# A row bound on the gathers and scatters of two routed layers in an audio tower on one Trainium2 core

## The chip, the core and the metric

The kernel is one program on one core of a Trainium2 chip. The metric is its device time in microseconds (us), from the first to the last instruction with the little that lies around it. One execution is also profiled; all stage times below are read from that one.

## What is computed

The reference is an audio tower on 64 clips of 33 frames (2112 tokens of 128 numbers): a windowed transform, then eight layers, each of which is added to the running sum `h`. The two layers that this change touches send each token to some of several small two-layer networks ("experts"):

```
# L1 ffn: 64 experts, each token goes to the 2 with the largest share
probs = jax.nn.softmax(logits, axis=-1)
vals, idx = jax.lax.top_k(probs, K)                 # K = 2
eh = jax.nn.silu(jnp.einsum('td,edf->tef', h, W1) + b1)      # 128 -> 512
eo = jnp.einsum('tef,efd->ted', eh, W2) + b2                 # 512 -> 128
moe = jnp.einsum('te,ted->td', combine, eo)
...
# L2 ffn: 8 experts, each token goes to 1
routes = jnp.argmax(probs, axis=-1)
h = jax.nn.gelu(xt @ w1 + bb1, approximate=False)
out = jnp.einsum('te,etd->td', onehot, y) * prob_max[:, None]
```

Only the chosen experts' results count, so the kernel computes those alone.

## The kernel before

Both layers are the function `moe`, called once with the key `sf` (64 experts, K = 2) and once with `gf` (8 experts, K = 1). Tokens are sorted by expert into slots, and slots are cut into tiles of `ST` = 128. A tile belongs to one expert, so an expert's last tile is filled only in part, and since the program can't know how the tokens will fall, it always runs the number of tiles that any routing could need: `NTILE` = 96 in the `sf` layer and 24 in the `gf` layer. There are K x 2112 real rows for them: 4,224 in 12,288 slots of `sf` (34%), and 2,112 in 3,072 slots of `gf` (69%).

A first block of `moe` computes the routing. Its last instructions, a chain on VectorE, make two index tables of int32 with a column of 128 for each tile: `take` (for each slot, the row of the token in the HBM tensor `token_rows`, `xs` in the code) and `give` (for each slot, the row of `expert_rows`, `ys`, that its result goes to). For an empty slot `take` is 0, so row 0 is fetched, and `give` is a row of its own behind the K x 2112 real ones, a trash row that nobody reads.

A second block runs the tiles, with every engine in its own program order and semaphores between them:

- SyncE loads the 514 KB of weights of tile j into `wb[:, j % 8]` (L1772), once tile j - 8 is done (`down`).
- GpSimd issues, for each j, an indirect DMA that gathers 128 rows of 512 bytes into `xi[:, j % 8]` (L2102), once the tile that held this buffer has been transposed (`turned`); and then, for tile d = j - 7 (`KEEP_RUN`), an indirect DMA that scatters the 128 rows of `yo[:, d % 8]` (L2107), once they are there (`y_ready`). So one gather and one scatter alternate, and a wait of either holds the other.
- TensorE transposes the gathered rows into `px` (L2131, which waits for the gather's landing, `taken`), and multiplies by the first weights into `ph` (L2139, 8 weight loads and matmuls as profiled) and the second into `po` (L2149, also 8).
- VectorE copies `px` to `xT` (L2199) and `po` to `yo` (L2205), ScalarE applies the activation (L2259, four a tile). VectorE also runs a small recurrence beside the `sf` tiles (L1637 to L1642), and in the `gf` layer a preparation of later weights (L2940, L2944).

Behind the last tile SyncE waits for all scatters and reads the rows back (`gk`, L2093), and VectorE and TensorE weigh and sum them. Semaphores of a finished stage are cleared on GpSimd (L98).

Of the kernel before, what the change touches and what calls it, by code (L numbers as in the profile page):

```python
# [5 lines left out]
F32 = mybir.dt.float32  # L6
# [3 lines left out]
ALU = mybir.AluOpType  # L10
# [5 lines left out]
D = 128  # L16
# [52 lines left out]
def unique(nc, name):  # L69

    return f"{name}_{nc.next_id()}"
# [1621 lines left out]


ST = 128
UN = 8
KEEP_RUN = 7

# [34 lines left out]
def moe(nc, cst, a, key, x, out, pre, F, act_fn, prob, capacity=None, code=None, shared=None, beside=None, late=False):  # L1733
# [7 lines left out]
    full = [TT, NTT, E]  # L1741
    w_dram = a[key + "_w"]
    xs = nc.dram_tensor(unique(nc, "token_rows"), [NT, D], F32, kind="Internal").ap()
    ys = nc.dram_tensor(unique(nc, "expert_rows"), [NTILE * ST if late else K * NT + NTILE * ST, D], F32, kind="Internal").ap()
    iota, iota16, low, index, tri, trash = (cst[n] for n in ("iota", "iota16", "low", "index", "tri", "trash"))

    def tile(t):
# [6 lines left out]
    with ExitStack() as ctx:  # L1754
# [19 lines left out]
        with ExitStack() as c1:  # L1774
# [173 lines left out]
            def _(dve):  # L1948
# [93 lines left out]
                if K == 2:  # L2042
# [1 line left out]
                                                op0=ALU.mult, op1=ALU.add))  # L2044
                    link(v.tensor_scalar(inv[:, 1, :], inv[:, 1, :], NTT - 0.5, -float(NTT), ALU.is_ge, ALU.mult))
                    link(v.tensor_tensor(inv[:, 2, :], inv[:, 2, :], inv[:, 1, :], ALU.add))
                link(v.tensor_scalar(take[:, :], inv[:, 2, :], -float(NTT), 0.0, ALU.add, ALU.max))
                if not late:
                    link(v.tensor_scalar(inv[:, 0, :], inv[:, 0, :], 0.0, None, ALU.is_equal))
                    link(v.scalar_tensor_tensor(out=inv[:, 1, :], in0=trash[:, 0:NTILE], scalar=float(K * NT + KB - 1), in1=inv[:, 0, :],  # L2050
                                                op0=ALU.add, op1=ALU.mult))
                    link(v.scalar_tensor_tensor(out=give[:, :], in0=inv[:, 1 + K, :], scalar=-float(KB), in1=inv[:, 1, :],
                                                op0=ALU.add, op1=ALU.add))

        with ExitStack() as c1:
            xi = sbuf(nc, c1, "xi", [ST, UN, D])
# [12 lines left out]
                stage(nc, "turned xT_ready up h_ready down y_ready shares_turned shares_kept"))  # L2069
            (weighed, added_up, dc) = c1.enter_context(stage(nc, "weighed added_up dve_chain"))  # L2070
            loaded = [s.sem for s in cst["y_back"]] if late else c1.enter_context(stage(nc, " ".join(f"loaded{g}" for g in range(NG))))
            pt = [t[:, b, :] for t in (px, ph, po) for b in range(2)]
            taken = [(s.sem, s.n) for s in x_in]
            given = [(s.sem, s.n) for s in y_out]
# [20 lines left out]

            @block.gpsimd
            def _(pool):
                for j in range(NTILE + KEEP_RUN):
                    if j < NTILE:
                        if j >= UN:  # L2100
                            pool.wait_ge(turned, j - UN + 1)
                        pool.indirect_dma_start(xi[:, j % UN, :], None, xs,  # L2102
                                                bass.IndirectOffsetOnAxis(ap=take[:, j:j + 1], axis=0)).then_inc(taken[j % UN][0], 16)
                    d = j - KEEP_RUN
                    if d >= 0 and not late:
                        pool.wait_ge(y_ready, d + 1)
                        pool.indirect_dma_start(ys, bass.IndirectOffsetOnAxis(ap=give[:, d:d + 1], axis=0), yo[:, d % UN, :],  # L2107
                                                None).then_inc(given[d % UN][0], 16)
                if late:
                    for j in range(NTILE - UN, NTILE):  # L2110
                        pool.wait_ge(*through(given, j))
                    for g, (t0, t1) in enumerate(groups):
                        for t in range(t0, t1):
                            pool.indirect_dma_start(gk[:, 0, t, :], None, ys,
                                                    bass.IndirectOffsetOnAxis(ap=place[:, t:t + 1], axis=0)).then_inc(loaded[g], 16)
# [1191 lines left out]
```

## Time and profile before

| | |
|---|---|
| median of 3 runs | 2192.21 us (2188.38 to 2197.41) |
| profiled execution: its own time / its span | 2194.47 us / 2192.5 us |
| TensorE, VectorE, ScalarE, GpSimd busy | 85%, 76%, 59%, 46% of the span |
| mean granted TensorE clock | 0.923 |
| gathers and scatters of the routed layers | 120 and 120, 0.99 and 1.00 us each on average on GpSimd |
| `sf` tiles: first gather issued / last scatter issued | 1164.05 us / 1411.68 us |
| `gf` tiles: the same | 1562.81 us / 1629.20 us |

The spans of an indirect DMA on GpSimd are the time in which that engine handles the instruction; its rows land later. "issue" as a releaser means that the engine waited for nothing that the profile shows. PEld is TensorE's weight load, which overlaps its matmuls.

### The profile page before, as it was taken

The numbers are of one execution on the slowest core, as the hardware profiler recorded it, in microseconds if no ns is written. First come the engines' busy times: TensorE is split into PE (matmuls) and PEld (weight loads), VectorE is DVE, ScalarE is ACT, GpSimd is POOL, SyncE is SP. The second block draws the span as 40 slices with busy tenths as digits, with TensorE's granted clock in tenths as the row PEclk, the third lists the DMA queues.
The fourth block names the chain that finished last, engine by engine and source line by source line (L and its number), as shares of the span: only waits on it lengthen the run. The fifth ranks groups of instructions, "written<-read, shape, count | busy, mean of one in ns | idle before, by whom it ended". The sixth has DMA issues, their size and how long they took to land. (4 is left out here: it accounts for less than half of the span.)

```text
span 2192.5 us, 49028 instructions
## 1 busy us (share of the span) xinstructions
PE 1853.0 (85%) x19401; PEld 1350.9 (62%) x19401; DVE 1665.2 (76%) x2535; ACT 1302.9 (59%) x2663; POOL 1006.3 (46%) x775
## 2 busy tenths in 40 slices
PE   7888888888888867897747887888688799999998
PEld 4444444444443333545537777767676599999997
DVE  3999999999999996678495443347544589989997
ACT  5777777776776655114334444343356488888886
POOL 1777777777677772110005777500350033333333
PEclk9899999999999999898668999999799699999999
DMA  3444444444444441520025888600750321111000
GB/s 128 148 130 130 126 150 129 130 131 125 126 131 144 135 133 49 129 43 1 17 97 155 268 258 251 189 10 5 246 157 14 149 85 63 70 59 66 16 4 23
DMA packets 91380, 242.16 MB, mean 110 GB/s; under 512 B 14800, under 2 KB 40000, under 8 KB 88720
## 3 DMA queue, kind: packets, MB, share of 16 engines
q1 hardware_dynamic: 82464, 218.66, 32.3%
q0 software_dynamic: 7680, 15.74, 3.0%
q10 hardware_dynamic: 1008, 4.62, 0.6%
q8 instruction: 154, 2.52, 0.5%
q14 instruction: 74, 0.61, 0.1%
HBM read 226.79 MB, written 12.19 MB: 109 GB/s over the span
## 5 line engine op out<-in xcount | busy, mean ns | idle before, releaser
L1099 POOL TENSOR_TENSOR dBu<-du,Bs 128x858 f32<-128x858 f32 (+1 forms) x240 | 589.7, 2459 | 212.8 <-DVE hst L1024 98.2
L568 PE MATMUL py<-hst,ident 128*128 128x429 f32 (+1 forms) x960 | 418.9, 568 | 94.8 <-DVE hst L1034 94.1
L1024 DVE TENSOR_TENSOR_SCAN hst<-dA,dBu 128x858 f32<-128x858 f32 (+1 forms) x240 | 457.7, 1907 | 19.3 <-ACT dA L873 15.8
L873 ACT ACTIVATE dA<-dt,negA 128x416 f32<-128x416 f32 (+1 forms) x480 | 269.4, 596 | 171.1 <-DVE hst L1024 168.4
L568 PEld LDWEIGHTS py<-hst,ident 128*128 128x128 f32 x960 | 185.8, 205 | 295.4 <-DVE hst L1034 167.7
L2855 POOL TENSOR_TENSOR hm<-h,mw 128x264 f32<-128x264 f32 x128 | 89.8, 701 | 391.2 <-DVE h L2836 391.2
L2102 POOL DMA_INDIRECT xi<-token_rows,take x120 | 118.8, 990 | 286.2 <-issue 278.0
L1034 DVE TENSOR_TENSOR hst<-hst,Cs 128x858 f32<-128x858 f32 (+1 forms) x240 | 246.9, 1029 | 0.0
L2259 ACT ACTIVATE eh<-ph,wb 128x128 f32<-128x128 f32 x480 | 136.3, 367 | 155.9 <-PE ph L2139 155.9
L2733 PE MATMUL pg<-hs,wh 128*128 128x66 f16 x6144 | 218.0, 193 | 5.8 <-issue 5.8
L2733 PE MATMUL pg<-xm,wi 128*128 128x66 f16 x6144 | 214.2, 195 | 4.8 <-issue 3.5
L2733 PEld LDWEIGHTS pg<-hs,wh 128*128 128x128 f16 x6144 | 203.9, 98 | 9.7 <-issue 6.3
L2733 PEld LDWEIGHTS pg<-xm,wi 128*128 128x128 f16 x6144 | 201.5, 98 | 9.3 <-issue 4.0
L2779 ACT ACTIVATE pg<-bz 128x1188 f32<-128x1188 f32 x128 | 149.1, 1165 | 6.2 <-PE pg L2728 2.2
L2107 POOL DMA_INDIRECT expert_rows<-yo,give x120 | 120.6, 1005 | 40.5 <-issue 32.6
L2205 DVE COPY yo<-po 128x128 f32<-128x128 f32 x120 | 34.9, 291 | 136.3 <-PE po L2149 136.1
L2139 PE MATMUL ph<-xT,wb 128*128 128x128 f32 x960 | 130.2, 280 | 2.8 <-DVE xT L2199 1.9
L2149 PE MATMUL po<-wb,eh 128*128 128x128 f32 x960 | 127.0, 276 | 0.0
L2826 DVE TENSOR_TENSOR prod<-z 128x528 f32<-128x528 f32 x128 | 111.3, 869 | 15.8 <-ACT z L2789 15.5
L2139 PEld LDWEIGHTS ph<-xT,wb 128*128 128x128 f32 x960 | 118.7, 194 | 4.0 <-DVE xT L2199 2.9
L2149 PEld LDWEIGHTS po<-wb,eh 128*128 128x128 f32 x960 | 117.4, 193 | 0.0
L2788 ACT ACTIVATE z<-pg,scale 128x528 f32<-128x528 f32 x128 | 88.1, 688 | 23.8 <-PE pg L2733 22.8
(487 smaller groups left out, 3209.4 us busy)
## 6 DMA issues: line engine op xcount, KB each, us to landing
wb<-sf_w SPq DMA_DIRECT2D x96, 514.0 KB, 5.0
Bs<-bc_rows SPq DMA_DIRECT2D x96, 429.0 KB, 4.6
Cs<-bc_rows SPq DMA_DIRECT2D x96, 429.0 KB, 3.5
mw<-route_weights SPq DMA_DIRECT2D x8, 2112.0 KB, 9.7
wb<-gf_w SPq DMA_DIRECT2D x24, 514.0 KB, 4.9
Bs<-bc_rows SPq DMA_DIRECT2D x24, 396.0 KB, 4.9
Cs<-bc_rows SPq DMA_DIRECT2D x24, 396.0 KB, 4.6
mb<-route_masks SPq DMA_DIRECT2D x8, 1088.0 KB, 12.4
```

The lines of the kernel that those rows point to most:

```text
L568: return nc.tensor.matmul(out, weight, moving, **kw)
L873: last = a(o, by_seq(dt[:, j % 2, h, 0:n])[:, :, 1:S], ACT.Exp, scale=negA[:, l, h * DST + k:h * DST + k + 1])
L1024: v.tensor_tensor_scan(hst[:, g % HR, 0:2 * n], dA[:, g % 2, 0:2 * n], dBu[:, g % 2, 0:2 * n], 0.0, ALU.mult, ALU.add).then_inc(h_ready, 1)
L1034: v.tensor_tensor(h, h, Cs[:, q % NBS, k % BG, 0:n].unsqueeze(1).broadcast_to([128, 2, n]), ALU.mult).then_inc(weighed, 1)
L1099: g_.tensor_tensor(dBu[:, g % 2, 0:2 * n].rearrange("p (a n) -> p a n", a=2), du[:, j % 2, :, 0:n], Bs[:, q % NBS, k % BG, 0:n].unsqueeze( ...
L2102: pool.indirect_dma_start(xi[:, j % UN, :], None, xs, bass.IndirectOffsetOnAxis(ap=take[:, j:j + 1], axis=0)).then_inc(taken[j % UN][0], 16)
L2107: pool.indirect_dma_start(ys, bass.IndirectOffsetOnAxis(ap=give[:, d:d + 1], axis=0), yo[:, d % UN, :], None).then_inc(given[d % UN][0], 16)
L2139: last = nc.tensor.matmul(ph[:, j % 2, f * ST:(f + 1) * ST], wb[:, j % UN, f * 128:(f + 1) * 128], xT[:, j % UN, :], start=True, stop=True)
L2149: last = nc.tensor.matmul(po[:, j % 2, 0:D], eh[:, j % 3, f, :], wb[:, j % UN, F + f * D:F + (f + 1) * D], start=(f == 0), stop=(f == FC - 1))
L2259: last = nc.scalar.activation(eh[:, j % 3, f, :], ph[:, j % 2, f * ST:(f + 1) * ST], act_fn, bias=wb[:, j % UN, W1 + W2 + f:W1 + W2 + f + 1])
L2733: return nc.tensor.matmul(pg[q][:, bank, c:c + CB], (wh if u else wi)[:, wp, q * HE + e, GO[z_] * D:(GO[z_] + 1) * D], rhs, start=False, s ...
L2779: a(pg[q][:, :, 0:PERB * CB], bz[:, q, :, :], ACT.Copy).then_inc(seeded[q], 1)
```

## The change

An empty slot's indices get 16384 added in both tables, which is above every row number, and both indirect DMAs get a bound (`bounds_check`: 2111 for the gather, K x 2112 - 1 for the scatter) with `oob_is_err=False`: rows whose index is above the bound are left out. `expert_rows` loses its trash rows. As the gather now leaves the empty slots' rows of `xi` as they were, `xi` is zeroed once before the tiles.

```
+SKIPPED = 16384.0
...
-    ys = nc.dram_tensor(unique(nc, "expert_rows"), [NTILE * ST if late else K * NT + NTILE * ST, D], F32, kind="Internal").ap()
+    ys = nc.dram_tensor(unique(nc, "expert_rows"), [NTILE * ST if late else K * NT, D], F32, kind="Internal").ap()
...
-                link(v.tensor_scalar(take[:, :], inv[:, 2, :], -float(NTT), 0.0, ALU.add, ALU.max))
-                if not late:
-                    link(v.tensor_scalar(inv[:, 0, :], inv[:, 0, :], 0.0, None, ALU.is_equal))
-                    link(v.scalar_tensor_tensor(out=inv[:, 1, :], in0=trash[:, 0:NTILE], scalar=float(K * NT + KB - 1), in1=inv[:, 0, :],
-                                                op0=ALU.add, op1=ALU.mult))
-                    link(v.scalar_tensor_tensor(out=give[:, :], in0=inv[:, 1 + K, :], scalar=-float(KB), in1=inv[:, 1, :],
-                                                op0=ALU.add, op1=ALU.add))
+                link(v.tensor_scalar(inv[:, 0, :], inv[:, 0, :], 0.0, SKIPPED, ALU.is_equal, ALU.mult))
+                v.scalar_tensor_tensor(out=take[:, :], in0=inv[:, 2, :], scalar=-float(NTT), in1=inv[:, 0, :], op0=ALU.add, op1=ALU.add)
+                link(v.scalar_tensor_tensor(out=give[:, :], in0=inv[:, 1 + K, :], scalar=-float(KB), in1=inv[:, 0, :],
+                                            op0=ALU.add, op1=ALU.add))
...
+            (cleared,) = c1.enter_context(stage(nc, "cleared"))
...
             @block.gpsimd
             def _(pool):
+                nc.gpsimd.memset(xi[:, :, :], 0.0).then_inc(cleared, 1)
+                pool.wait_ge(cleared, 1)
                 for j in range(NTILE + KEEP_RUN):
                     if j < NTILE:
                         if j >= UN:
                             pool.wait_ge(turned, j - UN + 1)
                         pool.indirect_dma_start(xi[:, j % UN, :], None, xs,
-                                                bass.IndirectOffsetOnAxis(ap=take[:, j:j + 1], axis=0)).then_inc(taken[j % UN][0], 16)
+                                                bass.IndirectOffsetOnAxis(ap=take[:, j:j + 1], axis=0),
+                                                bounds_check=NT - 1, oob_is_err=False).then_inc(taken[j % UN][0], 16)
                     d = j - KEEP_RUN
                     if d >= 0 and not late:
                         pool.wait_ge(y_ready, d + 1)
                         pool.indirect_dma_start(ys, bass.IndirectOffsetOnAxis(ap=give[:, d:d + 1], axis=0), yo[:, d % UN, :],
-                                                None).then_inc(given[d % UN][0], 16)
+                                                None, bounds_check=K * NT - 1, oob_is_err=False).then_inc(given[d % UN][0], 16)
```

In the order of the built program two places move. On GpSimd, at the head of the `sf` layer's tiles (`xi` is the gather's target, `expert_rows` the scatter's; ISA rows are semaphore clears), it stands before as

```order
L98 ISA x38
L2096 UNCONDITIONAL_BRANCH
L2102 DMA xi<-token_rows,take 128x128 x8
L2107 DMA expert_rows<-yo,give 16512x128
L2102 DMA xi<-token_rows,take 128x128
```

and in the change as

```order
L98 ISA x38
L2095 UNCONDITIONAL_BRANCH
L2097 MEMSET xi 128x1024
L2103 DMA xi<-token_rows,take 128x128 x8
L2109 DMA expert_rows<-yo,give 4224x128
L2103 DMA xi<-token_rows,take 128x128
```

The zeroing of all eight buffers comes ahead of the first gather, and the alternation behind it is as it was. These rows leave out what only sets a register: in the built program such an instruction, which holds the bound, now stands ahead of every one of the 240 indirect DMAs, and carries the wait that the DMA itself carried before.

On VectorE, at the end of the `sf` layer's routing block (`inv` is the scratch from which the tables are made), it stands before as

```order
L2046 TENSOR_TENSOR inv<-inv 128x96
L2047 TENSOR_SCALAR take<-inv 128x96
L2049 TENSOR_SCALAR inv<-inv 128x96
L2050 SCALAR_TENSOR_TENSOR inv<-trash,inv 128x96
L2052 SCALAR_TENSOR_TENSOR give<-inv 128x96
```

and in the change as

```order
L2046 TENSOR_SCALAR inv<-inv 128x96
L2047 TENSOR_TENSOR inv<-inv 128x96
L2048 TENSOR_SCALAR inv<-inv 128x96
L2049 SCALAR_TENSOR_TENSOR take<-inv 128x96
L2050 SCALAR_TENSOR_TENSOR give<-inv 128x96
```

Four instructions behind the last TENSOR_TENSOR on `inv` have become three.

## Rows read from the trace of the kernel before

**Rows 1.** Stages: busy time of each engine in three stretches

```profile
core 0: us, PE busy (x) PEld busy (x) DVE busy (x) ACT busy (x) POOL busy (x), PEclk, DMA share, GB/s
1175.00:1404.00 229.00, 188.31 (x1557) 176.84 (x1557) 91.76 (x343) 105.11 (x367) 174.66 (x179) 0.99 0.87 255
1562.00:1631.00 69.00, 58.02 (x461) 53.57 (x461) 35.60 (x76) 40.45 (x114) 51.68 (x48) 0.97 0.62 188
```

**Rows 2.** GpSimd in order of time: start, length; idle before and releaser

```profile
1164.05 1.17 POOL L2102 DMA_INDIRECT xi<-token_rows,take  x1 [100.10 <-issue]
...
1175.03 0.99 POOL L2107 DMA_INDIRECT expert_rows<-yo,give  x1 [1.07 <-DVE yo L2205]
1176.33 0.98 POOL L2102 DMA_INDIRECT xi<-token_rows,take  x1 [0.30 <-issue]
...
1400.92 0.99 POOL L2107 DMA_INDIRECT expert_rows<-yo,give  x1 [0.30 <-issue]
...
1405.45 0.97 POOL L2107 DMA_INDIRECT expert_rows<-yo,give  x1 [0.93 <-DVE yo L2205]
```

**Rows 3.** TensorE in order of time, 1202 to 1212 us

```profile
1202.42 0.27 PE L2131 MATMUL px<-ident,xi 128*128 128x128 f32 x1
...
1204.32 0.27 PE L2131 MATMUL px<-ident,xi 128*128 128x128 f32 x1
...
1206.22 0.27 PE L2131 MATMUL px<-ident,xi 128*128 128x128 f32 x1
...
1211.87 0.33 PE L2131 MATMUL px<-ident,xi 128*128 128x128 f32 x1 [3.60 <-DMA xi<-token_rows,take]
```

**Rows 4.** Waits from 1160 to 1400 us: total, times, longest

```profile
PEld px L2131 <- DMA xi<-token_rows,take: 52.9, 60, 3.8
```

**Rows 5.** DMA queues from 1170 to 1400 us (230 us), and issues

```profile
q1 hardware_dynamic: 12670, 46.32, 64.8%
q0 software_dynamic: 5683, 11.66, 21.5%
...
wb<-sf_w SPq DMA_DIRECT2D x88, 514.0 KB, 4.9
xi<-token_rows,take POOLq DMA_INDIRECT x92, 4.7
```

**Rows 6.** VectorE and TensorE at the border of routing and tiles

```profile
1160.06 0.21 DVE L2047 TENSOR_SCALAR take<-inv 128x96 int32<-128x96 f32 x1
1160.30 0.21 DVE L2049 TENSOR_SCALAR inv<-inv 128x96 f32<-128x96 f32 x1
1160.55 0.26 DVE L2050 SCALAR_TENSOR_TENSOR inv<-trash,inv 128x96 f32<-128x96 f32 x1
1160.84 0.26 DVE L2052 SCALAR_TENSOR_TENSOR give<-inv 128x96 int32<-128x96 f32 x1
...
1161.63 4.82 PE L133 MATMUL po<-ident 128*128 128x128 f32 x24 [4.34 <-PEq L1774]
```

**Rows 7.** Groups on GpSimd: busy, mean ns of one | idle before

```profile
L1080 POOL MEMSET whh<- 128x512 f32 x1 | 0.5, 527 | 0.0
...
L1077 POOL MEMSET edge<- 128x1 f32 x1 | 0.1, 104 | 0.0
```

**Rows 8.** SyncE's issue of weights: durations ns min/median/max

```profile
L1772 SPq MOVE wb<-sf_w x96: 29/29/42, 1133.4 to 1394.9; - x96
```

**Rows 9.** GpSimd, then VectorE, in the `gf` tiles in order of time

```profile
1584.46 0.99 POOL L2107 DMA_INDIRECT expert_rows<-yo,give  x1 [0.31 <-issue]
...
1605.46 1.90 POOL L2102 DMA_INDIRECT xi<-token_rows,take  x1 [0.30 <-PE px L2131]
```

```profile
1605.30 1.22 DVE L2944 TENSOR_TENSOR wi<-wf,wi 128x1024 f16<-128x1024 f32 x1
1607.20 1.22 DVE L2944 TENSOR_TENSOR wi<-wf,wi 128x1024 f16<-128x1024 f32 x1
```

**Rows 10.** Waits from 1560 to 1640 us

```profile
PE px L2131 <- DMA xi<-token_rows,take: 8.1, 7, 2.1
```

**Rows 11.** The gather over the whole span: durations ns min/median/max

```profile
L2102 POOL DMA_INDIRECT xi<-token_rows,take x120: 940/968/1898, 1164.0 to 1618.3; - x120
```

## The prediction

> **What bounds the kernel now.** I read the stages first, because the change touches only two stretches of the span. In the `sf` tiles (229 us of them in [rows 1]) TensorE is busy 82% of the time, GpSimd 76%, the DMA engines 87%, and no one number says who leads. The order of time on GpSimd does. From the first scatter at 1175.03 us to the scatter behind the last gather at 1400.92 us there are 88 pairs of one gather and one scatter: 225.9 / 88 = 2.57 us a pair, and it is made of 0.97 + 0.30 + 0.99 + 0.30 us [rows 2, 11], where 0.30 us is an idle time that recurs before nearly every one and has no releaser ("issue"). So GpSimd handles indirect DMAs without a pause. Its 76% is 100% with those gaps.
>
> TensorE, on the other hand, has time. Where rows are there it starts a tile every 1.90 us (1202.42, 1204.32, 1206.22), and then it waits 3.60 us for a gather [rows 3]; its wait for gathers is 52.9 us in the stretch [rows 4], near to 96 x (2.57 - 1.90) = 64 us. The `sf` tiles are paced by GpSimd's time for one instruction, and the next limit is TensorE at 1.90 us a tile. A third is close: the weights keep the sixteen DMA engines busy 64.8% of 230 us for 88 loads, 1.69 us a tile, and the indirect DMAs 21.5%, 0.54 us for one of the some 91 pairs [rows 5], together 2.23 us of 2.57.
>
> In the `gf` tiles GpSimd paces too, but only from about 1584 us on. TensorE is busy 58.0 of 69 us there [rows 1] and waits for gathers 8.1 us in all [rows 10].
>
> So the time of this change is decided by one number that the trace of before can't show: what GpSimd needs for an indirect DMA with a bound, of whose 128 indices only 44 (`sf`, 4,224 / 96) or 88 (`gf`) are in bounds.
>
> **The change part by part.**
>
> *Head of the tiles.* The zeroing of 128x1024 lies ahead of the first gather with nothing beside it that helps: TensorE's first transpose needs that gather. By the two MEMSET rows [rows 7] an element costs (0.527 - 0.104) / 511 = 0.83 ns, so 0.104 + 1023 x 0.00083 = 0.95 us, and one gap of 0.30 us: 1.25 us. VectorE ends its chain earlier: from the start of L2047 to the end of L2052 it takes 1.04 us [rows 6], and three instructions of this kind take 0.24 + 0.26 + 0.26 = 0.76 us, 0.28 us less, and the other engines enter the tiles 0.5 us behind that end. Net +1.0 us a layer, +2 us in both.
>
> *A register write before each DMA.* On SyncE a MOVE takes 29 ns [rows 8]. It costs nothing if GpSimd's sequencer does it while the previous DMA is handled, and 240 x 0.029 = 7.0 us if it adds to each gap, 6 us of that where GpSimd paces. A DMA that is released by a semaphore starts 0.28 us after it (1175.03 against the end of `yo`, and likewise at 1405.45 [rows 2]), as long as the gap between two that wait for nothing, so the sequencer seems not to be ahead. I take 5 us.
>
> *The DMA engines' load.* Rows moved fall to 34% in `sf`: 0.54 us a pair becomes 0.19, and the DMA engines' need falls from 2.23 to 1.88 us a tile. While GpSimd gives 2.57 us a tile, this alone buys nothing. It matters as the cover for a faster GpSimd: with it, a tile can come down to TensorE's 1.90 us, without it only to 2.23.
>
> *GpSimd's time for one instruction.* Call f the part of its 0.98 us (mean of 0.97 and 0.99) that goes with the number of rows actually issued. With f = 0 nothing changes. With f = 1 it would be 0.98 x 0.34 = 0.34 us in `sf`, and TensorE's 1.90 us would pace: 88 x 0.67 = 59 us less there, and up to 8 us in `gf` [rows 10]. No row shows a DMA with fewer rows, so f is open in both directions, a bound's test could cost as well. Two things lean on it. For a small f: a gather takes up to 1.90 us instead of 0.97 where VectorE's 1.22 us instructions with two inputs (L2944) run beside it [rows 9, 11]; something in it is held that is not the writing of rows' descriptors alone, and that stays. For a larger one: 128 rows on two sides in 0.97 us is 7.6 ns a row, as an instruction of 128x1 takes only 0.10 us [rows 7], so most of the 0.97 us is work that an almost empty instruction does not have. I take a third. Then an `sf` instruction takes 0.98 x (1 - 0.66 / 3) = 0.76 us, a pair 2 x (0.76 + 0.30) = 2.13 us, and 88 pairs save 88 x 0.44 = 39 us; in `gf` 0.98 x (1 - 0.31 / 3) = 0.88 us, and some 14 paced pairs save 14 x 0.20 = 3 us, of which I keep 2.
>
> A rule of the Trainium skill speaks against this (page DMA: Bandwidth & Descriptors, section Anatomy of one DMA): descriptor generation is a small part, and many descriptors can be emitted before their incremental cost is seen. By it f is near 0 and the sum would be that of the first rival below, +7 us; by the third that I took from the row it is -34 us. The same page names a fixed cost of some 2 us for a DMA's completion, which fewer rows would not shorten; the 4.7 us to landing in [rows 5] are in no conflict with it. On what holds the long gathers, SBUF — State Buffer, section Who interferes with whom, says that a VectorE instruction with two SBUF inputs blocks GpSimd's reads of SBUF, and here the trace agrees: 1.90 against 0.97 us.
>
> *Sum.* +2 (heads) +5 (register writes) -39 (`sf`) -2 (`gf`) = -34 us. The profiled execution took 2194.47 us (span 2192.5 and 2 around it), the median of the runs is 2192.21; the same difference on the median gives 2158 us. At the tail nothing is added: the last scatters wait for `yo` (0.93 us, [rows 2]), and SyncE reads back behind their landing as before.
>
> **The rivals.** About 0.5% (11 us) is what a measurement of this kernel tells from no change.
>
> *Nothing changes on GpSimd (f = 0).* The bytes go, but they were not the limit, and heads and register writes stay: +2 to +8, I take +7, 2199 us. For it: the load on the DMA engines is 87%, not 100%, and the rule above. Against it: the 7.6 ns a row. Chance 0.26.
>
> *The bound makes the instruction longer.* A test for each of 128 indices, or the loss of a form in which four rows of 512 bytes go as one packet (5683 packets for 11.66 MB are 2 KB each [rows 5]), adds d to each. 88 pairs and 14 in `gf` and the first 8 gathers: 0.1 us costs 0.1 x (176 + 28 + 8) = 21 us. On top of +7 it decides from d = 0.02 us on, at which the kernel is 11 us slower; with d = 0.2 us (1.6 ns an index) it is +49 us, 2241 us. For it: the pace hangs on this one instruction and nothing covers it. Against it: skipped rows save writes that are there now. Chance 0.31.
>
> *GpSimd gets faster, but the DMA engines don't get freer*, because skipped rows split packets: 2.23 us a tile would pace, 88 x 0.34 = 30 us less, -25 us with the rest, 2167 us. It lies within my own case.
>
> My case, GpSimd shorter, whatever the f between 0.1 and 1: chance 0.43, from 2192 + 7 - 67 = 2132 us to about 2181.
>
> **How the numbers follow.** The time is the likeliest case's, 2158 us; its own range is 2130 to 2181. For 8 in 10 the range has to take in f = 0 (up to 2203) and the slower case to d = 0.2: 2130 to 2245 leaves out about 0.03 below and 0.13 above. Faster by over 0.5% is my case, 0.43; the same is the first rival, 0.26; slower 0.31.
>
> **What would show it.** In the changed kernel's order of time on GpSimd: a MEMSET of about 0.95 us before the first gather; gathers and scatters in `sf` at 0.76 us for my case, 0.97 for the first rival, above 1.0 for the second; the gap still 0.30 or 0.33. The distance of two pairs in the middle of `sf` should be 2.13 us. The last 21 of 96 tiles are empty, by the number of tokens that each expert gets from the reference's inputs, so the instruction should be shortest there if it goes with the rows, and TensorE should run at 1.90 us. Bytes on queue 0 should fall to about 40% of 15.7 MB. TensorE's wait for gathers should fall from 52.9 us to some 20. The prediction is wrong if the instruction's time doesn't depend on the rows, or if it is longer with the bound whatever the rows.

## The result, and the profile after

The changed kernel took 2198.32 us (2192.67 to 2205.03) against 2192.17 us (2186.56 to 2199.86) for the kernel before, 20 executions of each: ratio 1.003, 95% interval 1.0021 to 1.0038. That is 6 us slower, inside the 0.5% that the prediction calls no change, and 40 us above the 2158 us that it gave. It was the first rival's time (2199 us), though not quite by the first rival's sum.

The page of the profile after shows that the rows did go. GpSimd's own row, the DMA totals, queue 0, and the two groups of indirect DMAs:

```profile
span 2196.8 us, 49270 instructions
PE 1852.0 (84%) x19401; PEld 1352.4 (62%) x19401; DVE 1665.2 (76%) x2533; ACT 1303.3 (59%) x2663; POOL 1016.7 (46%) x777
DMA packets 91382, 233.00 MB, mean 106 GB/s; under 512 B 16736, under 2 KB 42000, under 8 KB 88720
q0 software_dynamic: 7680, 6.58, 1.2%
L2109 POOL DMA_INDIRECT expert_rows<-yo,give x120 | 123.8, 1031 | 39.2 <-issue 27.5
L2103 POOL DMA_INDIRECT xi<-token_rows,take x120 | 124.3, 1036 | 37.7 <-issue 31.7
```

Before, queue 0 carried 7680 packets with 15.74 MB at 3.0% of the DMA engines. The bytes fell to 42%; the number of packets did not change at all. And an average gather or scatter takes *longer* than before: 1.04 and 1.03 us instead of 0.99 and 1.00.

The stages (answers to [rows 1]), the waits for gathers (to [rows 4]) and the queues of the `sf` tiles (to [rows 5]):

```profile
core 0: us, PE busy (x) PEld busy (x) DVE busy (x) ACT busy (x) POOL busy (x), PEclk, DMA share, GB/s
1175.00:1404.00 229.00, 181.68 (x1513) 170.31 (x1511) 89.82 (x334) 102.15 (x357) 176.32 (x173) 1.00 0.74 220
1562.00:1631.00 69.00, 58.89 (x458) 56.31 (x458) 35.30 (x76) 41.72 (x115) 49.64 (x46) 0.90 0.59 192
...
PEld px L2133 <- DMA xi<-token_rows,take: 59.7, 59, 2.9
...
q1 hardware_dynamic: 12632, 46.21, 67.0%
q0 software_dynamic: 5512, 4.28, 7.4%
...
wb<-sf_w SPq DMA_DIRECT2D x88, 514.0 KB, 4.3
xi<-token_rows,take POOLq DMA_INDIRECT x87, 3.5
```

The DMA engines' share fell from 0.87 to 0.74, queue 0's part of it from 21.5% to 7.4%, and a gather lands 3.5 us after its issue instead of 4.7. The transfers are fewer bytes and land sooner. Yet TensorE waits for gathers 59.7 us instead of 52.9, and fewer of its instructions fit into the same 229 us (1513 against 1557). Where the time sits is seen on GpSimd in order of time: the head of the tiles, two pairs from the middle, and the end, from the last gather on (answers to [rows 2]).

```profile
1159.22 0.95 POOL L2097 MEMSET xi<- 128x1024 f32 x1 [99.21 <-issue]
1161.06 1.23 POOL L2103 DMA_INDIRECT xi<-token_rows,take  x1 [0.90 <-POOL xi L2097]
...
1171.94 1.01 POOL L2109 DMA_INDIRECT expert_rows<-yo,give  x1 [0.53 <-issue]
...
1279.42 1.02 POOL L2103 DMA_INDIRECT xi<-token_rows,take  x1 [0.30 <-issue]
1280.75 1.02 POOL L2109 DMA_INDIRECT expert_rows<-yo,give  x1 [0.31 <-issue]
1282.07 1.02 POOL L2103 DMA_INDIRECT xi<-token_rows,take  x1 [0.30 <-issue]
1283.40 1.01 POOL L2109 DMA_INDIRECT expert_rows<-yo,give  x1 [0.31 <-DVE yo L2207]
...
1404.15 1.02 POOL L2103 DMA_INDIRECT xi<-token_rows,take  x1 [0.30 <-issue]
1405.48 1.02 POOL L2109 DMA_INDIRECT expert_rows<-yo,give  x1 [0.31 <-issue]
...
1410.83 0.98 POOL L2109 DMA_INDIRECT expert_rows<-yo,give  x1 [0.43 <-issue]
```

This order of time holds the prediction's own test. By the number of tokens that each expert gets, the last 21 of the 96 `sf` tiles have no row at all, and the instruction should have been shortest there if it went with the rows. The last gather (1404.15) takes 1.02 us, as do those in the middle; over the 21 empty tiles the mean is 1.022 us, over the filled ones from the tenth on 1.022 as well.

The durations of the gather, of the register write that now stands ahead of each, and of the scatter, over the whole span (answers to [rows 11]):

```profile
L2103 POOLq MOVE  x120: 29/29/35, 1160.2 to 1614.9; - x120
L2103 POOL DMA_INDIRECT xi<-token_rows,take x120: 995/1024/1675, 1161.1 to 1622.1; - x120
```

```profile
L2109 POOL DMA_INDIRECT expert_rows<-yo,give x120: 980/1016/1672, 1171.9 to 1634.4; - x120
```

Gathers went from a median of 0.97 to 1.02 us, scatters from 0.99 to 1.02. From the first scatter to the scatter behind the last gather it is 1405.48 - 1171.94 = 233.5 us for the same 88 pairs, 2.654 us a pair instead of 2.567, +7.7 us. The gaps are 0.30 to 0.31 as before: the register write is hidden. Laid out from the end of the chain that makes `give` to the read-back of `expert_rows` behind the last scatter, 252.9 us before (1161.10 to 1414.02) and 260.2 after (1157.18 to 1417.41):

| part of the `sf` tiles | before | after | difference |
|---|---|---|---|
| end of `give` to the first gather | 2.95 | 3.88 | +0.9 |
| first gather to first scatter | 10.98 | 10.88 | -0.1 |
| 88 pairs | 225.89 | 233.54 | +7.7 |
| scatter behind the last gather to the read-back | 13.10 | 11.93 | -1.2 |

The same stretch of the `gf` layer went from 72.8 to 74.7 us, +1.9, and VectorE's shorter chain returned 0.3 us a layer. These parts sum to about +9 us; the two profiled executions differ by 4.3 us, because in the one after everything ahead of the tiles happened to be 3.9 us shorter. The medians, +6 us, lie between.

### The profile page after: what moved, and what is told of

Its sections match the earlier page's. It is cut to its first block and busy times, and to the rows that moved or that the text cites. A ratio compares the mean times of both kernels' runs of the same rounds, so it can differ in the third digit from the quotient of the medians.

```text
span 2196.8 us, 49270 instructions
## 1 busy us (share of the span) xinstructions
PE 1852.0 (84%) x19401; PEld 1352.4 (62%) x19401; DVE 1665.2 (76%) x2533; ACT 1303.3 (59%) x2663; POOL 1016.7 (46%) x777
## 3 DMA queue, kind: packets, MB, share of 16 engines
q0 software_dynamic: 7680, 6.58, 1.2%
## 5 line engine op out<-in xcount | busy, mean ns | idle before, releaser
L2103 POOL DMA_INDIRECT xi<-token_rows,take x120 | 124.3, 1036 | 37.7 <-issue 31.7
```

Source lines behind the costliest of these rows:

```text
L2103: pool.indirect_dma_start(xi[:, j % UN, :], None, xs, bass.IndirectOffsetOnAxis(ap=take[:, j:j + 1], axis=0), bounds_check=NT - 1, oob_is_ ...
```

## Experiments

Behind each time stand, in brackets, its ratio to the kernel before on the same chip and the 95% interval of that ratio. Two kinds of chip occurred, two chips of each beside that of the result. On one kind the kernel before has a median of 2191 to 2193 us, as in the result above, on the other 2243 to 2245 us; an experiment is read only against its own chip. The first four kernels ran on one of the latter.

**1. The bound alone, with all rows moved.** The only edit on the kernel before is a bound that no index exceeds:

```diff
                         pool.indirect_dma_start(xi[:, j % UN, :], None, xs,
-                                                bass.IndirectOffsetOnAxis(ap=take[:, j:j + 1], axis=0)).then_inc(taken[j % UN][0], 16)
+                                                bass.IndirectOffsetOnAxis(ap=take[:, j:j + 1], axis=0),
+                                                bounds_check=NT - 1, oob_is_err=False).then_inc(taken[j % UN][0], 16)
...
-                                                None).then_inc(given[d % UN][0], 16)
+                                                None, bounds_check=K * NT + NTILE * ST - 1, oob_is_err=False).then_inc(given[d % UN][0], 16)
```

> The kernel before with a bound on both indirect DMAs that no index exceeds (trash rows, row 0 for empty slots and index tables as before, no zeroing): every one of the 128 rows still goes. Theory A, the bound's presence costs some 40 ns an instruction, whatever the rows: gathers about 1.02 and scatters 1.02 us in the sf tiles, a pair 2.65 us, +7 us in sf and +1 in gf, about 2200 us against 2192. Theory B, it is the skipping of rows that costs: 0.97 and 0.99 us, a pair 2.57 us, no change. Theory C, the bound costs more than 40 ns and the rows left out give part of it back: over 1.05 us an instruction, a pair over 2.70 us, over 2204 us.

**2. Every row of the gathers left out.** In the changed kernel all entries of `take` lie above the bound, so the experts compute on zeros:

```diff
-                v.scalar_tensor_tensor(out=take[:, :], in0=inv[:, 2, :], scalar=-float(NTT), in1=inv[:, 0, :], op0=ALU.add, op1=ALU.add)
+                v.scalar_tensor_tensor(out=take[:, :], in0=inv[:, 2, :], scalar=SKIPPED, in1=inv[:, 0, :], op0=ALU.add, op1=ALU.add)
```

> The changed kernel with every gather index above its bound, so that no gather moves a row (the tokens never reach the experts, whose results are those of zeros); scatters as in the change. Theory A (time by indices given, not by rows moved): gathers stay at 1.00 to 1.02 us, a pair at 2.65 us, 2198 us, although queue 0 loses the gathers' bytes. Theory C (time by rows moved): gathers fall below 0.95 us, and each 0.05 us is worth 4 us. Theory B (a skipped row costs extra): gathers above 1.05 us.

**3. The scatter alone.** The changed kernel with the gathers of before: no bound on them, no zeroing.

> Bound and left-out rows on the scatter alone; the gather as before, without zeroing. Theory A: gather 0.97, scatter 1.02 us, a pair 2.59 to 2.60 us, +2 to +3 us in sf, and -0.6 us at the heads: 2192 + 2 = 2194 us. If the effects of gather and scatter depended on each other (through the shared DMA queue) the gather would move from 0.97 too.

**4. Gathers of 64 indices.** In the changed kernel each gather takes partitions 0 to 63 only; rows 64 to 127 are not loaded.

```diff
-                        pool.indirect_dma_start(xi[:, j % UN, :], None, xs,
-                                                bass.IndirectOffsetOnAxis(ap=take[:, j:j + 1], axis=0),
+                        pool.indirect_dma_start(xi[0:64, j % UN, :], None, xs,
+                                                bass.IndirectOffsetOnAxis(ap=take[0:64, j:j + 1], axis=0),
```

> The changed kernel with gathers of 64 indices instead of 128: tokens in slots 64 to 127 of a tile are not gathered (zeros go through in their place). Theory A (an instruction's time goes with the number of indices that it is given): gather 0.5 to 0.65 us, a pair 2.2 to 2.3 us, some -33 us in sf, about 2160 us. If the time is nearly all fixed: gather 0.95 to 1.02 us, 2198 us.

Measured, before at 2243.2 us: 2256.52 (1.007, 1.0052 to 1.0088), 2262.03 (1.0074, 1.0051 to 1.0096), 2256.31 (1.0063, 1.0048 to 1.0078), 2260.1 (1.0078, 1.006 to 1.0096). The durations of the gather in the four, in this order, ns min/median/max:

```profile
L2102 POOL DMA_INDIRECT xi<-token_rows,take x120: 992/1024/1597, 1157.7 to 1676.4; - x120
```

```profile
L2103 POOL DMA_INDIRECT xi<-token_rows,take x120: 996/1027/1976, 1163.8 to 1683.4; - x120
...
q0 software_dynamic: 7680, 3.36, 0.6%
```

```profile
L2100 POOL DMA_INDIRECT xi<-token_rows,take x120: 940/973/2027, 1157.7 to 1676.7; - x120
```

```profile
L2103 POOL DMA_INDIRECT xi<-token_rows,take x120: 938/962/1727, 1159.6 to 1677.6; - x120
```

These four rows settle what GpSimd needs. With the bound a gather takes 1.02 to 1.03 us whether all 128 rows are moved (first), on average 44 (after) or none (second); in the third, which has the bound on the scatters alone, the gather is back at 0.97 and the scatter at 1.01. So an instruction with the bound takes 0.02 to 0.05 us longer, and the rows left out return nothing: f, the part that goes with the rows, is 0. Even half as many *indices* save only 0.06 us of 1.02. Queue 0 keeps its 7680 packets with 3.36 MB, when no gathered row is moved at all.

The times of these four are another matter. They are 13 to 19 us above their own chip's kernel before, where the longer instructions alone were expected to make +8 (1) or +2 (3). On this chip the `sf` tiles are not paced by GpSimd in the way of [rows 2]; I come back to it under 7.

**5. The changed kernel again, and the bound with reporting.** On a chip where before took 2191.93 us: the kernel before, the changed one, and the kernel of 1 with the bound's default, by which an index out of bounds is reported (there is none).

```diff
-                                                bounds_check=NT - 1, oob_is_err=False).then_inc(taken[j % UN][0], 16)
+                                                bounds_check=NT - 1).then_inc(taken[j % UN][0], 16)
```

> The kernel before itself, as a run with a trace of its own beside the kernels below: no difference. Its GpSimd rows (0.97 and 0.99 us, a pair 2.57 us) are the measure for the others of this call; if the sf tiles have waits here that its first trace did not have, they belong to the chip and not to a change.

> The changed kernel beside the kernel before on one chip, each with a trace. Theory A (the bound costs 40 ns an instruction and nothing is given back): +7 us in the sf pairs, +0.65 us at each head, -1 us at the tail, +6 us in all, 1.003 as before. If the four kernels of the first call were 0.6 to 0.8% slower for another reason (GpSimd waited there for yo up to 2.1 us), that wait should be seen in this trace and not in that of the kernel before.

> As the bound alone, but with out-of-bounds indices reported instead of left out (there are none). Theory A1, the check itself costs the 40 ns: 1.02 us an instruction again. Theory A2, the silent leaving-out is what costs: 0.97 and 0.99 us, no change.

Measured: 2191.3 (0.9993, 0.9979 to 1.0007), 2201.36 (1.0032, 1.002 to 1.0043), 2205.71 (1.0058, 1.0036 to 1.0079). The result repeats. The bound with all rows moved costs 14 us here: gathers 1.04, scatters 1.03 us at the median, 2.686 us a pair, 88 x 0.12 = 10.5 us in `sf` alone. So the slower kernel needs no rows left out to be explained. Nor is it the silent form that costs: with reporting a gather is no shorter, but 0.02 us longer than in the changed kernel.

**6. Is GpSimd the pace? A dose of idle work.** Three writes of 128x1 ahead of each scatter in the kernel before, then one write of 128x512 (on both kinds of chip):

```diff
                         pool.wait_ge(y_ready, d + 1)
+                        for i in range(3):
+                            nc.gpsimd.memset(pad[:, 3 * d + i:3 * d + i + 1], 0.0)
```

```diff
+                        nc.gpsimd.memset(pad[:, :], 0.0).then_inc(padded, 1)
```

> The kernel before with three 0.10 us MEMSETs of one column on GpSimd ahead of each scatter, and nothing else. If GpSimd's own time paces the sf tiles, each pair grows by 0.3 us: 88 x 0.3 = +26 us in sf and some +4 us in gf, 2192 + 30 = 2222 us (1.014). If the pace is set elsewhere, under +5 us.

> The kernel before with one MEMSET of 128x512 (0.53 us) on GpSimd ahead of each scatter. The first dose showed that 0.17 us of MEMSETs fit into the 0.30 us gap, with 0.16 us of idle time left before the DMA. Theory A (GpSimd paces, whatever it does counts): the gap of 0.30 becomes 0.53 + 0.16 us, +0.39 us a pair, 88 x 0.39 = +34 us in sf and 3 to 6 us in gf, 2230 us (1.018). If pace is set elsewhere: under +10 us.

> The large dose again (0.53 us of MEMSET on GpSimd ahead of each scatter), for a chip whose median is 2192 us: +0.39 us a pair, +34 us in sf and 3 to 6 us in gf, 2230 us, if GpSimd paces there. On a chip at 2243 us no change, as before.

Measured: the small dose 2194.54 us (1.0009, 0.9995 to 1.0023); the large one 2240.65 (0.9986, 0.9972 to 1.0) on a chip with 2244.56, and 2235.34 (1.0204, 1.0182 to 1.0227) on one with 2191.11. The small dose missed its expectation of +30 us, and the order of time says why:

```profile
1341.05 0.17 POOL L2109 MEMSET pad<- 128x1 f32 x3
1341.38 0.99 POOL L2110 DMA_INDIRECT expert_rows<-yo,give  x1 [0.16 <-issue]
```

The three writes take 0.17 us together and fill the gap, of which 0.16 us is left. Only 0.03 us a pair is new. The large dose does not fit:

```profile
1342.07 0.97 POOL L2104 DMA_INDIRECT xi<-token_rows,take  x1 [0.30 <-issue]
1343.04 0.54 POOL L2111 MEMSET pad<- 128x512 f32 x1
1343.75 1.00 POOL L2112 DMA_INDIRECT expert_rows<-yo,give  x1 [0.17 <-POOL pad L2111]
1345.05 0.97 POOL L2104 DMA_INDIRECT xi<-token_rows,take  x1 [0.30 <-issue]
```

It adds 0.54 + 0.17 - 0.30 = 0.41 us; the pair goes from 2.57 to 2.99 and the kernel gains 44 us, of which 88 x 0.42 = 37 lie in the `sf` tiles. So on this kind of chip GpSimd paces the `sf` tiles, as the prediction read it.

**7. The other kind of chip.** The kernel before, once more with its profile where before takes 2244.56 us:

> The kernel before once more, for a trace on the chip of this call. If its median here is 2243 us, as in the first call, the GpSimd waits for yo of the first call (50 us in 36 to 39 waits in sf) should be in this trace too; if it is 2192 us, the pair is 2.57 us as before.

It took 2239.83 us. The stages of the `sf` tiles and two waits of that trace:

```profile
1180.00:1440.00 260.00, 200.84 (x1465) 191.48 (x1466) 83.56 (x327) 99.06 (x348) 167.56 (x171) 0.88 0.73 216
...
POOL expert_rows L2107 <- DVE yo L2205: 56.7, 38, 2.1
...
PEld px L2131 <- DMA xi<-token_rows,take: 7.9, 5, 2.9
```

The granted clock is 0.88 there, between its two levels of 1.2 and 2.4 GHz, instead of 0.99, a pair takes 3.05 us, GpSimd waits 56.7 us for results to scatter, and TensorE waits for gathers hardly at all. The instructions on GpSimd are as long as elsewhere (0.97 and 0.99 us). In the trace with the large dose GpSimd's wait for those results is all but gone:

```profile
POOL pad L2111 <- DVE yo L2210: 2.1, 2, 1.8
```

The dose used up idle time, and so cost nothing there. Its pair is 2.99 us, as on the other kind of chip, and the granted clock from 1180 to 1400 us is 0.99 again, on the very chip that shows 0.88 without the dose. So the low clock is no fixed mark of these chips. Whether the low clock makes the long pairs there, or something else makes both, no run separates. Nor is it settled why the bound still cost 0.6 to 0.8% on such a chip: pairs are 3.16 to 3.19 us and the granted clock 0.87 to 0.89 in all four of 1 to 4, also where the gathers were no longer than before.

**8. Are the weights' transfers a second pace?** The kernel before, without and with the bound of 1, and with the experts' weights loaded for the first eight tiles only; the loads for the later tiles are left out:

```diff
-                for j in range(UN, NTILE):
-                    sp.wait_ge(down, j - UN + 1)
-                    load_weights(sp, j)
...
-                    pe.wait_ge(w_loaded[j % UN], 16 * (j // UN + 1))
+                    pe.wait_ge(w_loaded[j % UN], 16)
```

> The kernel before, with weights loaded for the first 8 tiles only and used again for all others (the other experts' weights are left out). If GpSimd paces: the pair stays at 2.57 us on a 2192 chip, no change in time; on a 2243 chip the pair falls from 3.05 to 2.57 us, -40 us, if it is the weights that GpSimd and TensorE wait for there, and stays at 3.05 if not.

> The same with the bound on both indirect DMAs that no index exceeds. With the weights out of the way GpSimd alone should pace on either chip: a pair of 2.65 against 2.57 us, +7 us in sf and +1 in gf against the run before this one.

Measured, before at 2191.11 us: 2194.74 (1.0019, 1.0007 to 1.0032) and 2200.9 (1.0039, 1.0023 to 1.0054). Without these loads the DMA engines' share from 1180 to 1400 us falls from 0.88 to 0.23, and it buys nothing: 2.573 us a pair. With the bound, and with all rows moved, the gather is again as long as in the changed kernel:

```profile
L2099 POOL DMA_INDIRECT xi<-token_rows,take x120: 992/1024/1634, 1160.6 to 1624.5; - x120
```

The pair is 2.658 us, and 88 x 0.085 = 7.5 us stand against the 6.2 measured between the two runs. The price of the bound does not come through the DMA engines. So on the kind of chip of the result the bound alone, with no row left out and nothing zeroed, makes a slowdown of the changed kernel's size.

**9. Fewer indirect DMAs.** If the number of instructions is what costs, their number has to fall. The kernel has a second form, `late`, that neither layer uses: results are stored in slot order by a plain DMA of ScalarE, and each token's rows are fetched at the end by `place`, here K x 22 = 44 gathers. For `sf` that is 96 + 44 = 140 indirect DMAs instead of 192, and one a tile beside TensorE. I extended it to K = 2 with the bound on its gathers:

```diff
-                            pool.indirect_dma_start(gk[:, 0, t, :], None, ys,
-                                                    bass.IndirectOffsetOnAxis(ap=place[:, t:t + 1], axis=0)).then_inc(loaded[g], 16)
+                            for k in range(K):
+                                pool.indirect_dma_start(gk[:, k, t, :], None, ys,
+                                                        bass.IndirectOffsetOnAxis(ap=place[:, k * NTT + t:k * NTT + t + 1], axis=0)
+                                                        ).then_inc(loaded[g], 16)
...
-                shared=(ws, c[:, 4:6], c[:, 6:7], total, DSH), beside=RecurTaps(nc, c1, taps))
+                shared=(ws, c[:, 4:6], c[:, 6:7], total, DSH), beside=RecurTaps(nc, c1, taps), late=True)
```

> sf tiles stored as they are by plain DMAs on ScalarE's queue (the code's own late form, extended to K = 2) instead of the scatter, and gathered by token at the end (44 gathers of 96 rows); the sf gather with the bound, gf as before. Instead of 192 indirect DMAs 140, of which 96 beside the tiles: GpSimd needs 1.32 us a tile and no longer paces. Tiles by TensorE at 1.90 us or the DMA engines at some 2.05 us: 96 x 2.05 = 197 against 248 us, -50; the 44 gathers at the end 44 x 1.25 = 55 us, of which 6 to 9 were there already, +47; 2189 us, between 2175 and 2200. If the pace of the tiles is not GpSimd's instructions, the loop keeps 2.57 us a tile and the kernel is at 2240 us.

> As the previous one, but the sf gather without bound or zeroing, all 128 rows fetched. With GpSimd out of the way the left-out rows should for once be worth something: DMA engines 1.69 + 0.27 + 0.27 = 2.23 us a tile by the rows of before against some 2.05, +17 us against the previous one. If the rows are not felt here either, the two are equal within 2 us.

Both are far slower than expected: 2515.64 us (1.1208, 1.1189 to 1.1226) with the bound and 2517.08 (1.1213, 1.119 to 1.1237) without, before at 2244.56. The waits of the first name the flaw, which is mine:

```profile
ACT eh L2270 <- DVE yo L2216: 384.6, 94, 4.7
```

ScalarE waited for tile j's result, to store it, before it began tile j+1's activations, some 4.1 us in each of 94 tiles. With that wait as the pace, the two say nothing on the rows. Put right, ScalarE stores the result of three tiles before:

```diff
-                        act.wait_ge(y_ready, j + 1)
-                        act.dma_start(ys[j * ST:(j + 1) * ST, :], yo[:, j % UN, :]).then_inc(given[j % UN][0], 16)
+                        for d in range(j - 3, j - 2) if j < NTILE - 1 else range(j - 3, NTILE):
+                            if d >= 0:
+                                act.wait_ge(y_ready, d + 1)
+                                act.dma_start(ys[d * ST:(d + 1) * ST, :], yo[:, d % UN, :]).then_inc(given[d % UN][0], 16)
```

> The version with fewer instructions again, but ScalarE stores tile j - 3 instead of tile j behind the activations of tile j. In the trace of the previous form ScalarE waited for yo 49 times (199 us) before it went on to the next activations, which made a tile 5.4 us long; that wait is gone here. If GpSimd's instructions pace the tiles (2.57 us a tile on a chip whose median is 2192 us), the tiles come down to 1.9 to 2.1 us, -45 to -60 us, and the 44 gathers at the end give back +47: 2175 to 2195 us on such a chip. If something else paces them (weights), the tiles keep their length and the kernel is slower by some 40 us. On a chip whose median is 2243 us, where GpSimd waits in the tiles of before, I expect little from the tiles and 2280 us.

It took 2178.92 us (0.9933, 0.9918 to 0.9948, before at 2191.11): faster than the kernel before and the changed one, on a chip of the kind of the result, and within what was expected. No run shows it on the other kind.

**10. Are left-out rows worth anything?** The same kernel once with and once without the bound and the zeroing, together on a chip with before at 2192.73 us:

> The kernel of e9 without the bound and without the zeroing: every sf gather moves all its 128 rows again. GpSimd's gather is then 0.97 us instead of 1.02, but GpSimd no longer paces there. If the left-out rows are worth something only where GpSimd does not pace (my theory), the DMA engines, whose share was 0.99 in the sf tiles of e9, now have 84 rows of 4 KB more for each of 96 tiles to move: 33 MB of bytes at the 305 GB/s seen there would be some 100 us of sixteen engines' time if nothing of it were free; from the busy shares (the gathers of before took about half of the 21.5% of 230 us for both, 0.27 us a tile, of which 66% goes) it is 0.17 us a tile, 16 us: 2195 us. Rival (the rows are worth nothing here either, since TensorE paces and the engines' share counts waiting): the same as e9, 2179 us, or 2 to 3 us faster by the zeroing's time.

> The kernel of e9 once more, on the same chip as e14: 2179 us, 0.993 of before. If this chip is one on which before's tiles are paced otherwise (median near 2243 us), it shows whether fewer instructions help there too: by GpSimd's time alone they would not, by TensorE's and the DMA engines' they would be equal to before within 0.5%.

Measured: without the bound 2209.09 us (1.0073, 1.0054 to 1.0093), with it 2176.55 (0.9934, 0.9914 to 0.9954). The rows that were worth nothing in the changed kernel are worth 32 us here. First the kernel with the bound: its gathers on GpSimd, the windows, and the queues from 1175 to 1330 us.

```profile
1251.32 0.99 POOL L2110 DMA_INDIRECT xi<-token_rows,take  x1 [0.90 <-PE px L2142]
1253.22 0.99 POOL L2110 DMA_INDIRECT xi<-token_rows,take  x1 [0.90 <-PE px L2142]
...
1175.00:1330.00 155.00, 155.00 (x1397) 155.00 (x1396) 85.25 (x323) 94.82 (x331) 84.19 (x85) 1.00 0.96 322
...
q1 hardware_dynamic: 11557, 42.27, 79.0%
q10 hardware_dynamic: 11518, 5.25, 11.7%
q0 software_dynamic: 2688, 2.07, 4.3%
...
wb<-sf_w SPq DMA_DIRECT2D x81, 514.0 KB, 5.1
```

GpSimd now idles 0.90 us before each gather, until TensorE has a buffer free, and TensorE is busy for all of the 155 us at one tile in 1.90 us. Then the kernel without the bound, same views:

```profile
1175.00:1330.00 155.00, 140.54 (x1215) 138.01 (x1214) 79.79 (x301) 82.54 (x288) 72.13 (x74) 0.98 1.00 296
...
q1 hardware_dynamic: 9914, 36.27, 66.1%
q0 software_dynamic: 2352, 4.81, 22.9%
q10 hardware_dynamic: 9850, 4.49, 10.0%
...
wb<-sf_w SPq DMA_DIRECT2D x70, 514.0 KB, 7.4
```

The gathers take 22.9% of the DMA engines instead of 4.3%, the share is 1.00, weights land after 7.4 us instead of 5.1, and only 70 tiles' weights are issued instead of 81: 155 / 70 = 2.21 us a tile against 155 / 81 = 1.91. For 96 tiles that is 29 us, nearly the whole difference. Expected were 16 us, and the term that was too small is the gathers' load on the DMA engines: 22.9% of 155 us for 70 tiles is 0.51 us a tile, where I had counted 0.27 (and the "84 rows of 4 KB" of that expectation are rows of 512 bytes, 4.1 MB in all and not 33).

What the kernel of 9 pays back is its end, where, behind a wait of 21.70 us for the last stores, 44 gathers follow one another on GpSimd:

```profile
1355.53 0.93 POOL L2124 DMA_INDIRECT gk<-expert_rows,place  x1 [21.70 <-DMA expert_rows<-yo]
1356.76 0.91 POOL L2124 DMA_INDIRECT gk<-expert_rows,place  x1 [0.30 <-issue]
...
1408.03 0.91 POOL L2124 DMA_INDIRECT gk<-expert_rows,place  x1 [0.30 <-issue]
```

From the first to the last start it is 52.5 us, 1.22 each. They gather 96 rows and take 0.91 us, another point on the nearly flat line.

## Why the prediction was wrong

The measured 2198 us lies outside the likeliest case's own 2130 to 2181 us. The wider range, to 2245 us, held it only because it took in the rivals. Both things that the prediction named as its refutation are there: the instruction's time doesn't depend on the rows, and it is longer with the bound.

**The bound of the stretch: right.** "The `sf` tiles are paced by GpSimd's time for one instruction" held on the chips of the result: a dose of 0.41 us a pair came through in full (6), and the load of the weights could be taken away without effect (8).

**The step that failed: "I take a third."** The likeliest case rested on f = 1/3, so 0.76 us an instruction and -39 us in `sf`. Measured, f = 0: 1.02 to 1.03 us with 128, about 44 or no rows moved, and `sf` pairs that take 7.7 us more. The reason given for a larger f was 7.6 ns a row, got by dividing 0.97 us by 128 because an instruction of 128x1 takes 0.10 us. That division assumed what it was to show; 0.10 us of another operation is no floor for an indirect DMA. With 64 indices instead of 128 the duration falls by 0.06 us, 0.9 ns an index (4). By a straight line through these two points, which is an estimate, some 0.9 of the 1.02 us is there however short the list is. The rule of the Trainium skill that the prediction set against itself (page DMA: Bandwidth & Descriptors, section Anatomy of one DMA: many descriptors can be emitted before their incremental cost is seen) was on the side of the measurement: 0.9 ns an index. The prediction's own argument for a small f, the gathers of 1.90 us, pointed the same way and was outweighed.

**The bound's own price.** The second rival gave it a size to be fitted, d; it measured 0.05 us for a gather and 0.03 for a scatter. The formula for 212 instructions gives 212 x 0.04 = 8 us, and the 88 pairs alone showed +7.7. By the rival's own point of decision (d = 0.02 us on top of +7) the kernel should have been slower by over 0.5%. It was not, because the +7 underneath was too large, and the tail was shorter:

- *Register writes, +5:* under 1 us. The MOVE takes the 29 ns of [rows 8], but the gaps of 0.30 us stayed at 0.30 to 0.31. The argument that the sequencer is not ahead was wrong, or the gap has room: three small writes fitted into it too (6).
- *Heads, +1.0 a layer:* +0.9 in the `sf` table, less 0.3 from the shorter chain. The zeroing took the 0.95 us worked out, but began 2.04 us behind the end of `give`, where the first gather before began at 2.95; and its semaphore then took 0.90 us instead of a gap of 0.30.
- *The tail, "nothing is added":* -1.2 us. The last scatters, with no gather between them, take 0.98 us (1410.83), as they took 0.97 before (1405.45, [rows 2]), and they wait less for `yo`. That their tiles are empty is not why they are shorter: the scatter of an empty tile at 1405.48, right behind a gather, takes 1.02.

So +7.7 - 1.2 + 0.6 in `sf` and +1.6 in `gf` make about +9 in the profile, +6 by the medians: the first rival's time by half of the second rival's mechanism.

**The DMA engines: right in what decided, unproven in the rest.** "While GpSimd gives 2.57 us a tile, this alone buys nothing": the share fell from 0.87 to 0.74 and nothing came of it. "The DMA engines' need falls from 2.23 to 1.88 us a tile" could not be seen in this pair of kernels. In 10, where GpSimd no longer paced, a tile took 2.21 us without the bound and TensorE's 1.90 with it. That is the prediction's picture of a cover for a faster GpSimd, worth 29 us. That 2.21 is so close to 2.23 is in part luck: that kernel stores by plain DMAs instead of scatters, and its terms are 1.46 us for the weights, 0.51 for the gathers and 0.22 for the stores, against the prediction's 1.69 for the weights and 0.54 for a gather with its scatter.

**Packets.** The prediction read 5683 packets for 11.66 MB as four rows of 512 bytes in one packet, and feared that skipping would split them. The trace after contradicts it: 7680 packets before and after. 240 DMAs with 16 engines make 3840 shares, and 3840 is half of 7680: each share is one packet with its 8 rows, 4 KB, and one small one (15.74 MB / 3840 = 4.1 KB leaves nothing else for it). In the page after, 1936 more packets are under 512 B and 2000 more under 2 KB than before (14800 and 40000). (The second count includes the first.) Both are, to the unit, the numbers of shares with no row and with at most three rows left, counted from the tokens that each expert gets with partition p on engine 8 x (p // 64) + (p // 4) mod 8; with eight adjacent partitions to an engine they would be 2188 and 2244. The first assignment is that of the Trainium skill (page DMA: Bandwidth & Descriptors, section The descriptor swizzle), and the trace agrees with it. A row left out is thus taken from its packet, and a packet without rows still goes.

## What to carry to other kernels

Before making a transfer smaller, ask whether it is the transfer or the engine issuing it that paces: an order of time with equal distances on the issuing engine, while the DMA engines are below full, says that it is the issuing engine. Smaller transfers then return nothing here; fewer instructions (192 to 140) returned 0.67%, but only together with the rows left out, and without that the kernel was 0.73% slower. A fixed cost can't be told from a cost per element by dividing one row; measure a second size of the same operation, or hold the gain back. And a saving that shows nothing today may be what carries the next change: the bound costs 6 us in one schedule and saves 32 us in another, so test the two together.

## Not expected of the hardware

- In these tiles a gather of 128 rows of 512 bytes holds GpSimd 0.97 us, with a bound 1.02 to 1.03 whatever is left out, 1.04 with reporting, and 0.96 with a bound and 64 indices.
- The idle 0.30 us ahead of an indirect DMA isn't lost for other work: with writes of 0.17 us in it 0.16 us was left, so the two came only 0.03 us further apart.
- One kernel takes 2192 us on some chips and 2243 on others, with most of the extra time in these tiles (3.05 us a pair against 2.57) at a granted clock of 0.88 instead of 0.99, and the clock is 0.99 there too once GpSimd has 0.54 us more to do in each pair. What sets this off stays open, as does the 0.6 to 0.8% that the bound costs there.
